# Attention's two stores per sequence, issued by SP among its page requests instead of by GpSimd

## The chip, the cores and the metric

One core of a Trainium2 chip runs the whole program. The metric is the device time of one execution in microseconds. The kernel before took 2566.42 us (median of 3 runs, 2566.22 to 2566.6).

## The reference, cut to what matters

The input x has 64 sequences of 32 tokens and 512 features. Four residual layers follow each other: a linear layer with one of eight weights per sequence, two LoRA layers, and an attention layer. Only the last is touched here. Shortened:

```
q = rope(rmsnorm(x @ Wq.T))        # 32 heads of 128
k = rope(rmsnorm(x @ Wk.T))        # 8 heads
v = x @ Wv.T                       # 8 heads
k_all = concat(k_cache[block_table], k)   # 16 pages of 32 keys + 32 own keys = 544 keys
v_all = concat(v_cache[block_table], v)
probs = softmax(where(valid, q @ k_all.T / sqrt(128), -1e30))
o = probs @ v_all                  # per sequence 128 x (32 heads * 32 tokens)
x = x + o.reshape(64, 32, 4096) @ Wo.T
```

## The kernel before

The attention layer is built by `qkv_attention_and_output` (L1998) from three parts whose programs run one after the other on every engine: `qkv`, `attention` (L1285) and `output_projection` (L1729). Each engine has its own hand-written order of instructions; engines meet only at semaphores.

**Attention.** The sequences s = 0 to 63 are worked off in pairs: `in_pairs` writes the body once for the first pair, once as a loop over pairs 1 to 30, and once for the last pair (i = 31). Each sequence has 8 units, one for each key head; u counts units over all sequences, j within a pair. In a unit TensorE computes the scores of unit u + 2 (`scores`, L1433, six matmuls in three passes of a split fp32), the outputs of unit u - 4 (`outputs`, L1675: eight matmuls with cached values at L1687, two matmul halves with own values at L1690), and the transposes of the probabilities of unit u (`transpose`, L1658). In every fourth unit, the transposes are followed by one of `p_own` (L1670), which first waits for the masked scores of unit u + 2 on VectorE; in every eighth also by the sums' transpose (L1672), so that L1672 marks the end of a sequence's 8 units. VectorE gathers (L1592), masks and takes the maximum (L1403), splits keys and queries into high and low parts (L1378), copies the own probabilities (`copy_own`, L1600), inverts the sums (`invert`, L1607) and copies four heads of outputs out of PSUM (`copy_o`, L1615, which counts `o_ready`, two per sequence). The second of a sequence's two copies is in unit 5 of the next sequence. ScalarE has the exponentials (L1383), the high parts (L1372) and the copies of the transposes (L1558).

**Who asks for what.** SP runs `sync` (L1458): for each sequence 16 requests for key pages of 128 KB (L1350), in four pieces of four pages, each piece once `lo_done` tells that the same buffer's piece of two sequences before has been split. Pieces are split in units 7 (of the sequence before), 0, 2, 3 and 4, so the last piece is asked for after unit 4 and the next sequence's first after unit 7. GpSimd runs `gpsimd` (L1475): for each sequence the queries (L1479, 512 KB), the own keys (L1485), the own values (four requests, L1497, after `pv_done` of unit 3), the value pages as four indirect DMAs of 512 KB each (L1503), and then `store(s - 1)` (L1507): wait for `o_ready`, store the outputs of the sequence before (L1509, 512 KB, 128 rows of 4 KB), wait for `inv_ready`, store its reciprocal sums (L1512, 4 KB).

**Output projection.** Its SP program (L1771) follows attention's on SP. It first waits until four sequences of each parity are stored and until `lo_done` is 6 * 63 (L1790), which is in unit 4 of sequence 61, and then asks for the reciprocal sums of the first tile (`load_inv(0, 0)`, L1778, broadcast to 128 partitions, 1 MB) and for the weights of heads 0 to 3 (`load_w`, L1785, 256 KB each); at `lo_done` 6 * 64, unit 4 of sequence 62, for the first half tile of outputs (`load_o(0, 0)`, L1773, 1 MB) and the weights of heads 4 to 9. The work on these is put into attention's last pair on ScalarE and VectorE by unit number (`HI_AT_STEP`, `LO_AT_STEP`, L1720): weight 0 gets its high part (L1859) on ScalarE at step 6 after that unit's copy of transposes, and its low part (L1863) on VectorE at step 7; the first half tile is scaled at steps 9 to 12 (L1880), split at 10 to 15, and weights 4 to 7 follow at 14 and 15. Step 6 of the last pair is unit 6 of sequence 62. In program order the low part of weight 0 on VectorE stands ahead of `copy_own`, `invert`, `gather` and `mask_and_max` of step 8. The remaining weights wait for `w_split`, eight heads behind.

Of the kernel before, what the change touches and what calls it, by code (L numbers as in the profile page):

```python
# [33 lines left out]
DH, HQ, HK = 128, 32, 8  # L34
# [31 lines left out]


Programs = namedtuple("Programs", "sync gpsimd scalar vector tensor")
Ahead = namedtuple("Ahead", "sync scalar vector tensor")
Kept = namedtuple("Kept", "xt_hi xt_lo w_stage w_loaded after w_hi w_lo w_hi_done w_split")  # L70
Done = namedtuple("Done", "lo_done s_done masked gathered t_done pv_done")
Both = namedtuple("Both", "ident ident_ready step x_stored ps_s ps_pt ps_o ps_y ps_t mm_done normed_ready rotated_ready out_ready stored v_stored")
# [1212 lines left out]
def attention(nc, m, place, both, pool_sems, done, out_ahead, k_pages, v_pages, table, lens, key_at, q_t, k_own, v_own, o_t, inv_t):  # L1285
# [163 lines left out]
    def tensor_ahead(pe, j):  # L1449
# [3 lines left out]
        if j == STEPS:  # L1453

            pe.wait_ge(both.normed_ready, ALL_STEPS - 2)
            scores(pe, 0, 1, 1)

    def sync(sp):  # L1458
        def load_k(s, p):

            for c in PIECE_TURN:
                if c in CACHED:
                    if later(s, 2):
                        sp.wait_ge(lo_done, PIECES * (s - 2) + PIECE_TURN[c])
                    load_pages(sp, s, p, c)

        def pair(i, last):

            if not last:
                for p in range(2):  # L1470
                    load_k(2 * i + 2 + p, p)

        in_pairs(sp, NSEQ // 2, pair)

    def gpsimd(pool):  # L1475
        def load_q(s, p):
            if later(s, 2):
                pool.wait_ge(lo_done, PIECES * (s - 2) + PIECE_TURN[PIECE_Q])
            pool.dma_start(q_raw[p][:, :], q_t[bass.ds(s, 1)].rearrange("s d g x -> s d (g x)"))\  # L1479
                .then_inc(k_loaded[p][PIECE_Q], 16)  # L1480

        def load_own_k(s, p):
            if later(s, 2):
                pool.wait_ge(lo_done, PIECES * (s - 2) + PIECE_TURN[PIECE_OWN])
            pool.dma_start(k_raw[p][:, NPP, :], k_own[bass.ds(s, 1)]).then_inc(k_loaded[p][PIECE_OWN], 16)  # L1485

        def load_own_v(s, p):

            if later(s, 2):
                pool.wait_ge(pv_done, HK * (s - 1))  # L1490
            rows = v_own[bass.ds(s * SEQ, SEQ), :].rearrange("k (g u d) -> k g u d", g=HK // OG, u=OG)
            for u in range(OG):
                if u == 1:
                    pool.tensor_copy(rows_now[:, p, :], row_sb[:, bass.ds(s * (NPP // PPP), NPP // PPP)])\
                        .then_inc(rows_copied, 1)
                    pool.wait_ge(rows_copied, s + 1)
                pool.dma_start(vo_sb[p][u * SEQ:(u + 1) * SEQ, :, u, :], rows[:, :, u, :])\  # L1497
                    .then_inc(own_v_loaded[p], 16)

        def load_v(s, p):  # L1500

            for c in range(NPP // PPP):
                pool.indirect_dma_start(  # L1503
                    v_sb[p][:, c, :], None, v_pages.rearrange("n k x -> (n k) x"),
                    bass.IndirectOffsetOnAxis(ap=rows_now[:, p, c:c + 1], axis=0)).then_inc(v_loaded[p], 16)

        def store(s, p):  # L1507
            pool.wait_ge(o_ready, (HK // OG) * (s + 1))
            pool.dma_start(o_t[bass.ds(s, 1)], o_sb[:, p, :, :].rearrange("p h q -> p (h q)"))\  # L1509
                .then_inc(o_stored[p], 16)  # L1510
            pool.wait_ge(inv_ready, s + 1)
            pool.dma_start(inv_t[bass.ds(s, 1)].rearrange("s (h q) -> (s h) q", h=HK), inv_sb[:, p, :])\  # L1512
                .then_inc(inv_stored[p], 16)

        for p in range(2):
            pool.wait_ge(both.stored[p], 16 * (STEPS // 2) * (NB - 2))
        load_q(0, 0)
        pool.wait_ge(both.stored[0], 16 * ((STEPS // 2) * (NB - 2) + NT // 2 + 1))
        pool.wait_ge(rows_ready, PPP + 2)
        load_own_k(0, 0)  # L1520
        for p in range(2):
            pool.wait_ge(both.v_stored[p], 16 * STEPS // 2)
        pool.wait_ge(both.mm_done, ALL_STEPS)
        pool.memset(mask[:, :, NKEY:NALL], 0.0).then_inc(zeroed, 1)
        load_q(1, 1)
        load_own_k(1, 1)
        pool.memset(vo_sb[0][:, :, :, :], 0.0).then_inc(zeroed, 1)
        pool.wait_ge(zeroed, 2)
        load_own_v(0, 0)
        load_v(0, 0)  # L1530
        for p in range(2):
            pool.wait_ge(both.stored[p], 16 * ALL_STEPS // 2)
        pool.memset(vo_sb[1][:, :, :, :], 0.0).then_inc(zeroed, 1)
        pool.wait_ge(zeroed, 3)

        def pair(i, last):


            for p in range(2):
                s = 2 * i + p  # L1540
                if not last:
                    load_q(s + 2, p)
                    load_own_k(s + 2, p)
                if not (last and p):
                    load_own_v(s + 1, 1 - p)
                    load_v(s + 1, 1 - p)
                if later(s, 1):
                    store(s - 1, 1 - p)

        in_pairs(pool, NSEQ // 2, pair)  # L1550
        store(NSEQ - 1, 1)

    def scalar(act):
        def copy_pt(u, j):
# [102 lines left out]
    def tensor(pe):  # L1657
# [37 lines left out]
        def pair(i, last):  # L1695
# [9 lines left out]
            if last:  # L1705
# [2 lines left out]

        in_pairs(pe, NSEQ // 2, pair)

    return Ahead(sync_ahead, scalar_ahead, vector_ahead, tensor_ahead), Programs(sync, gpsimd, scalar, vector, tensor)

# [7 lines left out]
LO_AT_STEP = {7: ["w0"], 8: ["w1"], 9: ["scale0"], 10: ["scale1"], 11: ["scale2"], 12: ["scale3"], 13: ["o0"], 14: ["o1", "o2"],  # L1722
              15: ["o3", "w2", "w3"], 16: ["w4", "w5", "w6", "w7"]}
HEADS_AHEAD = 8
HALF_1_AT, HALF_1_HI_AT, HALF_1_LO_AT = 9, 11, 14
TILE_1_AT, TILE_1_INV_AT, TILE_1_SCALE_AT, TILE_1_SPLIT_AT = 13, 19, 23, 28


def output_projection(nc, m, base, both, pool_sems, done, x_in, o_t, inv_t, w, x_out):  # L1729
# [38 lines left out]

        return SPT * (n + 1) if isinstance(n, int) and n < 2 else n + 1 + FIRST_TILE_PARTS - 2

    def sync(sp):  # L1771
        def load_o(t, half):
            sp.dma_start(o_sb[half][:, :, :, :].rearrange("p s h q -> p s (h q)"),  # L1773
                         o_t[bass.ds(t * SPT, SPT), :, half * HH * SEQ:(half + 1) * HH * SEQ]
                         .rearrange("s d n -> d s n")).then_inc(o_loaded[half], 16)

        def load_inv(t, half):
            sp.dma_start(inv_sb[:, :, :],  # L1778
                         inv_t[bass.ds(t * SPT, SPT), half * HH * SEQ:(half + 1) * HH * SEQ]
                         .unsqueeze(0).to_broadcast([P, SPT, HH * SEQ])).then_inc(inv_loaded, 16)  # L1780

        def load_w(h):
            if h >= len(stage):
                sp.wait_ge(w_split, h - len(stage) + 1)
            sp.dma_start(stage[h % len(stage)][:, :], w[h // WG][:, h % WG, :]).then_inc(w_loaded[h % len(stage)], 16)  # L1785

        for p in range(2):
            sp.wait_ge(inv_stored[p], 16 * 4)
            sp.wait_ge(o_stored[p], 16 * 4)
        sp.wait_ge(done.lo_done, PIECES * (NSEQ - 1))  # L1790
        load_inv(0, 0)
        for h in range(WG):
            load_w(h)
        sp.wait_ge(done.lo_done, PIECES * NSEQ)
        load_o(0, 0)
        sp.wait_ge(done.s_done, HK * (NSEQ - 1))
        for h in range(WG, HEADS_AHEAD + 2):
            load_w(h)
        sp.wait_ge(scaled, count(0))
        load_inv(0, 1)  # L1800
        sp.wait_ge(done.s_done, HK * NSEQ)
        load_o(0, 1)
        for h in range(HEADS_AHEAD + 2, HQ):
            load_w(h)
            if h == TILE_1_AT:
                sp.wait_ge(split_done, count(0))
                load_o(1, 0)
            if h == TILE_1_INV_AT:
                sp.wait_ge(scaled, count(1))
                load_inv(1, 0)  # L1810
        sp.wait_ge(w_split, HQ)
        sp.dma_start(x_sb[:, :], x_in[0:P, :]).then_inc(x_loaded, 16)
        for p in range(2):
            sp.wait_ge(inv_stored[p], 16 * NSEQ // 2)
            sp.wait_ge(o_stored[p], 16 * NSEQ // 2)

        def pair(i, last):
            for p in range(2):
                t = 2 * i + p
                if not (last and p):  # L1820
                    for half in range(2):
                        if half or later(t, 1):
                            sp.wait_ge(split_done, count(2 * t + half))
                            load_o(t + 1, half)
                            sp.wait_ge(scaled, count(2 * t + half + 1))
                            load_inv(t + 1, half)
                sp.wait_ge(y_ready, t + 1)
                sp.dma_start(x_out[bass.ds(t * P, P), :], y_sb[:, :]).then_inc(y_stored, 16)
                if not (last and p):
                    sp.dma_start(x_sb[:, :], x_in[bass.ds((t + 1) * P, P), :]).then_inc(x_loaded, 16)  # L1830

        in_pairs(sp, NT // 2, pair)
        sp.wait_ge(y_stored, 16 * NT)
# [164 lines left out]
def qkv_attention_and_output(nc, pool_sems, base, shared, both, kept, w_all, lens_tok, inv_freq, step_pos, norm_w, k_pages, v_pages, table, lens, key_at,  # L1998
# [3 lines left out]
    with ExitStack() as ctx:  # L2002
# [17 lines left out]
        with nc.Block(no_gpsimd_drain=True) as block:  # L2020
            @block.sync
            def _(sp):
                proj.sync(sp)
                att.sync(sp)
                out.sync(sp)

            @block.gpsimd
            def _(pool):
# [117 lines left out]
```

## Time and profile before

| | |
|---|---|
| median of 3 runs | 2566.42 us |
| profiled execution | 2564.78 us, span of the core 2563.2 us |
| mean granted TensorE clock | 0.989 |
| TensorE matmul busy | 2422.7 us, 95% |
| VectorE, ScalarE, GpSimd busy | 1777.9, 1606.1, 600.5 us |
| DMA moved | 536.84 MB, mean 209 GB/s |

The profile is one execution. A share of busy time says how full an engine is, not whether it sets the end; for that one reads the chain of waits and the waits by engine. A row of the timeline gives the start, the length, the engine, the line, what is written from what, and in brackets how long the engine was idle before it and what is named as the releaser. "PEld" is TensorE's weight load; "SPq" and "POOLq" are instructions of the queue or sequencer.

### The profile page before, as it was taken

What the parts mean: (1) busy time and instruction counts of PE and PEld (TensorE: products, weight loads), DVE (VectorE), ACT (ScalarE), POOL (GpSimd) and SP (SyncE); (2) the same over time, 40 slices, a digit from 0 to 9 for tenths busy, and PEclk for the clock granted to TensorE, in tenths of its full rate; (3) what the DMA queues carried; (4) which work ended last, traced back from release to release, by engine and by line L of the source; (5) the groups of instructions that cost most, each with busy time, mean ns of one, the idle gap of its engine ahead of it and who ended that gap; (6) DMA issues with size and microseconds to landing.
All of it is one profiled execution on the core that took longest, in us unless ns stands there. A gap on an engine that the chain in (4) does not pass through costs nothing.

```text
span 2563.2 us, 54764 instructions
## 1 busy us (share of the span) xinstructions
PE 2422.7 (95%) x16070; PEld 2185.1 (85%) x16071; DVE 1777.9 (69%) x3668; ACT 1606.1 (63%) x3341; POOL 600.5 (23%) x896
## 2 busy tenths in 40 slices
PE   6899999999999899999999999999999999899999
PEld 4688788888888689999999999999999989788887
DVE  5454439989998777777777777777777777744443
ACT  3233348778777777777777777777777777511111
POOL 1200040000000143444443444443444443000000
PEclk9899999999999899999999999999999999999999
DMA  6622323333334598888788778888887887766564
GB/s 222 177 85 57 128 107 103 99 100 115 99 98 132 159 302 267 267 264 273 270 280 274 267 264 267 278 271 276 274 267 262 273 271 255 278 218 211 209 210 148
DMA packets 377209, 536.84 MB, mean 209 GB/s; under 512 B 49698, under 2 KB 263394, under 8 KB 374306
## 3 DMA queue, kind: packets, MB, share of 16 engines
q1 hardware_dynamic: 304994, 311.62, 38.5%
q0 software_dynamic: 70016, 221.30, 24.8%
q10 hardware_dynamic: 2112, 2.89, 0.4%
q8 instruction: 38, 0.62, 0.1%
q14 instruction: 49, 0.40, 0.0%
HBM read 437.35 MB, written 98.30 MB: 209 GB/s over the span
## 4 chain that ended last, share of the span: by engine, by line
PE 51%; another core or an unknown queue 4%; issue 4%; DVE 4%; ACT 1%; DMA 1%; DVEq 0%; SPq 0%; ACTq 0%
PE both_ps_o L1687 13%; PE both_ps_s L105 9%; PE both_ps_s L103 9%; PE both_ps_s L104 8%; PE both_ps_pt L1664 6%; PE both_ps_o L1690 3%; DVE att_prob L1403 2%; PE both_ps_s L1670 1%; ACT att_prob L1383 1%; DVE att_p_own L1592 0%; DMA out_w_stage<-in_wo 0%; DVE out_w_lo L1863 0%; DMA out_inv<-inv_t 0%; DVE att_shift L1403 0%
## 5 line engine op out<-in xcount | busy, mean ns | idle before, releaser
L1687 PE MATMUL both_ps_o<-att_pt,att_v 128*128 128x128 f32 x4096 | 539.2, 274 | 0.0
L1383 ACT ACTIVATE att_prob<-att_prob,att_shift 128x544 f32<-128x544 f32 x512 | 384.2, 750 | 238.1 <-DVE att_shift L1403 218.1
L1687 PEld LDWEIGHTS both_ps_o<-att_pt,att_v 128*128 128x128 f32 x4096 | 504.0, 191 | 0.0
L1403 DVE CUSTOM_DVE_ANT_0 att_prob<-both_ps_s,att_mask 128x544 f32<-128x544 f32 x512 | 364.1, 711 | 0.3 <-issue 0.2
L103 PE MATMUL both_ps_s<-att_k_hi,att_q_hi 128*128 128x272 f32 x1024 | 339.9, 332 | 6.0 <-DVE att_k_lo L1378 5.0
L1378 DVE TENSOR_TENSOR att_k_lo<-att_k_raw,att_k_hi 128x1024 fp32r<-128x1024 f32 (+1 forms) x320 | 338.0, 1056 | 2.0 <-ACT att_k_hi L1372 1.9
L1558 ACT ACTIVATE att_pt<-both_ps_pt 128x512 f32<-128x512 f32 x512 | 296.8, 580 | 60.7 <-remote 60.1
L1664 PE MATMUL both_ps_pt<-both_ident,att_prob 128*128 128x128 f32 x2048 | 309.2, 274 | 6.2 <-ACT att_prob L1383 4.6
L1592 DVE TENSOR_REDUCE att_p_own<-att_prob 128x32 f32<-128x32 f32 x512 | 89.7, 175 | 324.5 <-remote 159.7
L105 PE MATMUL both_ps_s<-att_k_hi,att_q_lo 128*128 128x272 f32 x1024 | 297.4, 290 | 0.0
L104 PE MATMUL both_ps_s<-att_k_lo,att_q_hi 128*128 128x272 f32 x1024 | 295.3, 288 | 0.0
L1372 ACT ACTIVATE att_k_hi<-att_k_raw 128x1024 fp32r<-128x1024 f32 (+1 forms) x320 | 293.2, 917 | 0.0
L1497 POOL DMA_DIRECT2D att_vo<-v_own x256 | 140.1, 547 | 649.8 <-PE both_ps_o L1690 587.2
L1503 POOL DMA_INDIRECT att_v<-in_v_pages,att_rows_now x256 | 251.9, 984 | 85.9 <-issue 85.9
L1664 PEld LDWEIGHTS both_ps_pt<-both_ident,att_prob 128*128 128x128 f32 x2048 | 242.5, 142 | 6.8 <-ACT att_prob L1383 4.8
L1912 ACT ACTIVATE out_o_hi<-out_o 128x2048 fp32r<-128x2048 f32 x30 | 57.6, 1920 | 265.8 <-DVE out_o L1934 265.8
L103 PE MATMUL both_ps_s<-out_w_hi,out_o_hi 128*128 128x512 f32 x512 | 202.4, 395 | 8.3 <-DVE out_w_lo L1863 4.6
L103 PEld LDWEIGHTS both_ps_s<-att_k_hi,att_q_hi 128*128 128x128 f32 x1024 | 194.8, 190 | 16.3 <-issue 8.8
L105 PE MATMUL both_ps_s<-out_w_hi,out_o_lo 128*128 128x512 f32 x512 | 201.6, 394 | 0.0
L104 PE MATMUL both_ps_s<-out_w_lo,out_o_hi 128*128 128x512 f32 x512 | 201.0, 393 | 0.0
L1690 PE MATMUL both_ps_o<-att_pto,att_vo 128*128 128x128 f32 x1024 | 198.5, 276 | 1.8 <-DVE att_pto L1600 1.8
L104 PEld LDWEIGHTS both_ps_s<-att_k_lo,att_q_hi 128*128 128x128 f32 x1024 | 195.9, 191 | 0.0
(214 smaller groups left out, 5035.5 us busy)
## 6 DMA issues: line engine op xcount, KB each, us to landing
att_k_raw<-in_k_pages SPq DMA_DIRECT2D x1024, 128.0 KB, 4.0
q_t<-qkv_out_t SPq DMA_DIRECT2D x128, 256.0 KB
att_q_raw<-q_t POOLq DMA_DIRECT2D x64, 512.0 KB, 7.2
o_t<-att_o POOLq DMA_DIRECT2D x64, 512.0 KB, 6.9
out_inv<-inv_t SPq DMA_DIRECT2D x32, 1024.0 KB
out_o<-o_t SPq DMA_DIRECT2D x32, 1024.0 KB, 6.6
both_w_stage<-in_w_qkv SPq DMA_DIRECT2D x12, 1024.0 KB, 5.3
l_w_stage<-in_w SPq DMA_DIRECT2D x8, 1024.0 KB, 7.6
```

What stands on the lines that cost most here:

```text
L103: pe.matmul(out, xh, wh, start=start, stop=False)
L104: pe.matmul(out, xh, wl, start=False, stop=False)
L105: return pe.matmul(out, xl, wh, start=False, stop=stop)
L1372: act.activation(hi, raw, ACT.Copy).then_inc(hi_done, 1)
L1378: dve.tensor_tensor(lo, raw, f32(hi), ALU.subtract).then_inc(lo_done, 1)
L1383: act.activation(prob[:, b, :], prob[:, b, :], ACT.Exp, bias=shift[:, b:b + 1], scale=-1.0, accum_out=total[:, j // HK, j % HK:j % HK + 1] ...
L1403: dve.tensor_tensor_reduce(out=prob[:, b, :].rearrange("p (a n) -> p a n", a=2), in0=ps_s[:, j % 2, :, 0:HALF], in1=mask[:, j // HK, :].re ...
L1503: pool.indirect_dma_start(v_sb[p][:, c, :], None, v_pages.rearrange("n k x -> (n k) x"), bass.IndirectOffsetOnAxis(ap=rows_now[:, p, c:c + ...
L1558: act.activation(pt_sb[:, j % OG, :, :], ps_pt[:, j % 2, :, :], ACT.Copy).then_inc(pt_ready, 1)
L1664: mm = pe.transpose(ps_pt[:, j % 2, c, :], prob[:, j % NB_P, c * P:(c + 1) * P], ident[:, :])
L1687: pe.matmul(out, v_sb[p][:, c, h * DH:(h + 1) * DH], pt_sb[:, j % OG, c, :], start=(c == 0), stop=False)
L1690: pe.matmul(out, vo_sb[p][:, g % 2, j % OG, :], pto_sb[:, g % 2, :], start=False, stop=True).then_inc(pv_done, 1)
```

## The change

`store` moves out of `gpsimd` and is written for any engine. SP calls it in attention's pair body: after the page requests for sequence 2i + 2 + p it stores sequence 2i - 2 + p, also in the last pair, where there are no page requests. GpSimd's calls go. The stores of the last two sequences go into SP's program of the output projection: that of sequence 62 after `load_o(0, 1)`, that of sequence 63 after the weight of head 15.

```
+    def store(eng, s, p):
+
+        eng.wait_ge(o_ready, (HK // OG) * (s + 1))
+        eng.dma_start(o_t[bass.ds(s, 1)], o_sb[:, p, :, :].rearrange("p h q -> p (h q)")).then_inc(o_stored[p], 16)
+        eng.wait_ge(inv_ready, s + 1)
+        eng.dma_start(inv_t[bass.ds(s, 1)].rearrange("s (h q) -> (s h) q", h=HK), inv_sb[:, p, :]).then_inc(inv_stored[p], 16)
+
     def sync(sp):
...
         def pair(i, last):
 
-            if not last:
-                for p in range(2):
+            for p in range(2):
+                if not last:
                     load_k(2 * i + 2 + p, p)
+                if later(i, 1):
+                    store(sp, 2 * i - 2 + p, p)
...
                 if not (last and p):
                     load_own_v(s + 1, 1 - p)
                     load_v(s + 1, 1 - p)
-                if later(s, 1):
-                    store(s - 1, 1 - p)
-
         in_pairs(pool, NSEQ // 2, pair)
-        store(NSEQ - 1, 1)
...
+LAST_STORE_AT = 15
...
-    def sync(sp):
+    def sync(sp, store):
...
         sp.wait_ge(done.s_done, HK * NSEQ)
         load_o(0, 1)
+        store(sp, NSEQ - 2, 0)
         for h in range(HEADS_AHEAD + 2, HQ):
             load_w(h)
+            if h == LAST_STORE_AT:
+                store(sp, NSEQ - 1, 1)
```

## Rows read from the trace of the kernel before

**Rows 1.** The page, busy us, share of the span, instructions.
```profile
PE 2422.7 (95%) x16070; PEld 2185.1 (85%) x16071; DVE 1777.9 (69%) x3668; ACT 1606.1 (63%) x3341; POOL 600.5 (23%) x896
```

**Rows 2.** Waits between 930 and 2150 us: us in total, times, longest.
```profile
POOL att_vo L1497 <- PE both_ps_o L1690: 564.7, 59, 10.7
DVE att_p_own L1592 <- remote: 156.8, 54, 3.5
PE both_ps_s L1670 <- DVE att_shift L1403: 69.4, 55, 1.4
```

**Rows 3.** Timeline of GpSimd in one sequence: fourth indirect DMA, stores, queries.
```profile
1521.21 0.94 POOL L1503 DMA_INDIRECT att_v<-in_v_pages,att_rows_now  x1 [0.30 <-issue]
1522.15 0.60 POOL L1509 DMA_DIRECT2D o_t<-att_o  x1
1522.74 0.56 POOL L1512 DMA_DIRECT2D inv_t<-att_inv  x1
1523.30 0.56 POOL L1479 DMA_DIRECT2D att_q_raw<-q_t  x1
```

**Rows 4.** Timeline of TensorE and VectorE, the same sequence and the marks of the one before.
```profile
1503.76 0.27 PE L1672 MATMUL both_ps_s<-both_ident,att_total 128*8 128x128 f32 x1
...
1521.05 0.29 PE L105 MATMUL both_ps_s<-att_k_hi,att_q_lo 128*128 128x272 f32 x1
...
1523.32 0.19 DVE L1592 TENSOR_REDUCE att_p_own<-att_prob 128x32 f32<-128x32 f32 x1 [2.33 <-remote]
...
1524.20 0.33 PE L1670 MATMUL both_ps_s<-both_ident,att_p_own 128*128 128x128 f32 x1 [1.31 <-DVE att_shift L1403]
1524.36 0.27 PE L1672 MATMUL both_ps_s<-both_ident,att_total 128*8 128x128 f32 x1
```

**Rows 5.** The chain of waits, start us and us, one sequence before.
```profile
1500.63 2.06 another core or an unknown queue
```

**Rows 6.** Timeline of TensorE: the marks of the last two sequences.
```profile
2173.83 0.27 PE L1672 MATMUL both_ps_s<-both_ident,att_total 128*8 128x128 f32 x1
...
2191.10 0.27 PE L1672 MATMUL both_ps_s<-both_ident,att_total 128*8 128x128 f32 x1
```

**Rows 7.** Line 989 between 500 and 870 us: SP's stores of queries in the projection.
```profile
L989 SPq DMA_DIRECT2D q_t<-qkv_out_t x90: 372/372/376, 500.6 to 784.4; - x90
```

**Rows 8.** Timeline of SP and VectorE around SP's last page requests of a sequence.
```profile
1516.99 2.38 SPq L1350 DMA_DIRECT2D att_k_raw<-in_k_pages  x4
1517.50 0.69 DVE L1615 COPY att_o<-both_ps_o 128x512 f32<-128x512 f32 x1
1526.17 1.37 SPq L1350 DMA_DIRECT2D att_k_raw<-in_k_pages  x3
```

**Rows 9.** Timeline of SP in the last pair.
```profile
2146.83 0.39 SPq L1778 DMA_DIRECT2D out_inv<-inv_t  x1
2147.28 2.32 SPq L1785 DMA_DIRECT2D out_w_stage<-in_wo  x4
2166.95 0.38 SPq L1773 DMA_DIRECT2D out_o<-o_t  x1
```

**Rows 10.** Timeline of VectorE, ScalarE and TensorE in the last pair.
```profile
2168.01 0.69 DVE L1615 COPY att_o<-both_ps_o 128x512 f32<-128x512 f32 x1
2173.21 0.62 ACT L1859 ACTIVATE out_w_hi<-out_w_stage 128x512 fp32r<-128x512 f32 x1
2174.47 0.28 DVE L1600 COPY att_pto<-both_ps_s 128x128 f32<-128x128 f32 x1
2175.59 0.39 PE L1690 MATMUL both_ps_o<-att_pto,att_vo 128*128 128x128 f32 x2
2178.99 0.69 DVE L1880 TENSOR_TENSOR out_o<-out_o,out_inv 128x512 f32<-128x512 f32 x1
```

**Rows 11.** Window 2173 to 2181 us: length, busy by engine, clock, DMA share, GB/s.
```profile
2173.00:2181.00 8.00, 7.73 (x68) 7.47 (x67) 6.99 (x18) 6.80 (x15) 0.00 (x0) 1.00 1.03 393
```

**Rows 12.** Line 1785 between 2167.3 and 2169.2 us: heads 4 to 7, issue to landing.
```profile
DMA to landing us min/median/max: 6.4/8.5/10.8
```

More of the change, by code:

```diff
@@ L68 @@
 Programs = namedtuple("Programs", "sync gpsimd scalar vector tensor")
-Ahead = namedtuple("Ahead", "sync scalar vector tensor")
+Ahead = namedtuple("Ahead", "sync scalar vector tensor store", defaults=[None])
 Kept = namedtuple("Kept", "xt_hi xt_lo w_stage w_loaded after w_hi w_lo w_hi_done w_split")
@@ L1505, in load_v @@
                     bass.IndirectOffsetOnAxis(ap=rows_now[:, p, c:c + 1], axis=0)).then_inc(v_loaded[p], 16)
[L1507 to L1513, printed above, removed]
         for p in range(2):
@@ L1709, in tensor @@
         in_pairs(pe, NSEQ // 2, pair)
-    return Ahead(sync_ahead, scalar_ahead, vector_ahead, tensor_ahead), Programs(sync, gpsimd, scalar, vector, tensor)
+    return Ahead(sync_ahead, scalar_ahead, vector_ahead, tensor_ahead, store), Programs(sync, gpsimd, scalar, vector, tensor)
 HH = HQ // 2
@@ L2024, in _ @@
                 att.sync(sp)
-                out.sync(sp)
+                out.sync(sp, ahead.store)
             @block.gpsimd
```

## The prediction

> **What bounds the kernel now.** I read the busy shares first: TensorE is busy 2422.7 us, 95% of the span, GpSimd 600.5 us, 23% [rows 1]. The reader should see that GpSimd's share alone promises nothing: work taken from an engine with three quarters of its time free only helps if something waits for that work.
>
> Second, the waits inside attention, 930 to 2150 us [rows 2]. GpSimd waits 564.7 us for TensorE at its own-value requests, about 9.6 us in each of 59 sequences, so it is not behind. TensorE waits 69.4 us in 55 places, always the same: once per sequence, at L1670. VectorE waits 156.8 us in 54 places for a releaser that the profile can't name.
>
> Third, the timeline of one such place [rows 4]. The last score matmul of the unit is at 1521.05 and should be done by 1521.34, but VectorE, which waits for exactly that, starts at 1523.32, 2.0 us later; TensorE then waits 1.31 us for VectorE's mask. The chain of waits puts 2.06 us of the same kind on the path one sequence earlier [rows 5]. So TensorE's completions reach the others late, once per sequence, and the sequence takes 1524.36 - 1503.76 = 20.60 us from mark to mark [rows 4]. The last sequence, in which no value pages are asked for, takes 2191.10 - 2173.83 = 17.27 us [rows 6]; it lacks two units' scores, some 0.75 us each by the spacing of the six matmuls, so 18.8 us is what a sequence takes without the stall. The stall is worth 20.6 - 18.8 = 1.8 us, in 60 sequences about 108 us: the largest thing this change could touch.
>
> Whose stall is it? The late completions arrive in the last stretch of GpSimd's four indirect DMAs and shortly after: the fourth is at 1521.21 to 1522.15, then come the two stores, and VectorE is released at 1523.32, as the queries' request starts at 1523.30 [rows 3, 4]. In the last sequence GpSimd still issues its stores, without indirect DMAs, and there is no stall [rows 6]. I take the indirect DMAs as the cause and the store as a bystander.
>
> **The change part by part.**
>
> *GpSimd loses two requests per sequence,* 0.60 + 0.56 = 1.16 us [rows 3], 64 times, 74 us in all. All lie in front of a 9.6 us wait [rows 2], so on the path they are worth 0. What follows them, the queries and own keys, is asked for 1.16 us earlier; these buffers are used two sequences later, nobody waits. If the cover were gone, it would be 1.16 us a sequence. The value pages are asked for at the same instant as before, since they hang on `pv_done`, so the stall stays where it is. Bounds of what the absence of the stores does to the stall: from 0 to the 1.16 us for which they lie in it. I take 0, by the last sequence, where stores alone stall nothing.
>
> *SP gains the two requests per sequence.* The nearest row is SP's store of 256 KB in the projection, 0.37 us, 90 times alike [rows 7]; twice that is 0.75 us of SP per sequence. SP's fourth piece is asked for from 1516.99 to 1519.37; the second output copy ends at 1518.19, so the wait for `o_ready` is already over when SP gets there, and its next page request that I can see waits for unit 7, about 1525 to 1526 [rows 8]. The store at 1519.4 to 1520.2 therefore lies in 5 us of idle SP: 0 on the path. Queued behind it are the next key pages, which are used more than a sequence later. Had the order been store first, the pages would wait for unit 5. In the projection TensorE's completions are not late beside 90 such stores, so I price SP's stores in the middle of the indirect DMAs at 0 too; no row shows this overlap, so the bounds are from -0.2 us (fewer requests for GpSimd's queue) to +0.3 us a sequence (the stall is pushed out by part of SP's 0.37 us), that is -12 to +18 us over 60.
>
> *Data.* The 512 KB of outputs go out on SP's queue during the values' transfer in place of behind it, so the values land some 1.3 us later (0.52 MB at 393 GB/s, rows 11). They are needed only in unit 4 of the next sequence, well over 5 us after. 0.
>
> *The last pair is where the order costs.* SP now has `store(60)` and `store(61)` ahead of all its output projection work. `store(61)` waits for the second output copy of sequence 61, 2168.01 + 0.69 = 2168.70 [rows 10]. Behind this wait stand the first reciprocal sums and the weights of heads 0 to 3, which before were asked for at 2146.83 to 2149.60 [rows 9]: 22 us later than before. They are wanted soon: ScalarE takes weight 0 at 2173.21 [rows 10]. New times on SP: outputs store at 2168.8, sums at 2169.3, `load_inv` at about 2170.1, weight 0 at 2170.6. Ahead of and with weight 0 on that queue are 0.52 + 1.05 + 0.26 = 1.83 MB, and GpSimd's last value pages, 2.1 MB, start at the same time. Together 3.93 MB at 393 GB/s [rows 11] are 10.0 us, from about 2168.6: 2178.6, plus some 0.3 us to the landing. The rows of before give the same another way: heads 4 to 7 stood behind a 1 MB load on this queue with the same values beside it and took 6.4 to 10.8 us [rows 12]; with 0.52 MB more ahead and a start 1.9 us later than 2166.95, weight 0 corresponds to head 6, at about 2179. I take 2179.1.
>
> What waits for it: ScalarE's high part of weight 0; then on VectorE its low part, and behind that in program order `copy_own`. From the start of the high part to the end of `copy_own` is 2174.75 - 2173.21 = 1.54 us, and TensorE wants that copy at 2175.59 [rows 10], so there is 0.8 us of slack. The delay of TensorE is 2179.1 + 1.54 - 2175.59 = 5.0 us. All engines shift behind it. The next need, scaling the first half tile, was at 2178.99 [rows 10] and goes to 2184; `load_o(0, 0)` needs 0.79 + 1.05 = 1.84 MB after weight 0, 4.7 us, 2183.8: just in time. Bounds: if SP's queue got all the DMA bandwidth, weight 0 would land at 2175.4 (1.83 MB at 393 GB/s after 2170.6) and cost 1.4 us; if it waits like head 7, 10.8 us after 2170.6, 7.4 us.
>
> *The last two stores* join SP's queue between loads that already keep the DMA engines full, with the same bytes as before; SP waits for neither copy by more than 1 us. 0, at most +1.
>
> **Sum.** 0 + 0 + 0 + 5.0 + 0 = +5.0 us on the profiled execution: 2564.78 to 2569.8, its span 2563.2 to 2568.2. The median of the runs lies 1.6 us above that execution, so 2566.42 + 5.0 = 2571.4.
>
> **What the Trainium skill says against it.** "Trainium Kernel Development and Optimization", Key Constraints: requests from SP, ScalarE and GpSimd run on the same 16 DMA engines, and the choice of issuer only saves the issuing sequencer's time. By that rule alone, 1.16 us saved on an idle GpSimd, the sum would be 0 and not +5; it leaves out the place in SP's order. "SBUF — State Buffer", "SBUF: two separate sides", warns of the opposite: descriptors that GpSimd writes starve while VectorE holds the shared port, and SP's requests are free of that, which speaks for a gain; here GpSimd's two requests take 0.60 and 0.56 us with VectorE busy beside them, and nothing waits for them.
>
> **The rivals.**
> A, forecast: the stall unchanged, weight 0 late. +5, by itself +1.4 to +7.4. 60%.
> B, faster: the store is part of the stall. For it: VectorE is released 0.02 us after the sums' store ends [rows 3, 4]. If the completions come through 0.6 us earlier, 60 x 0.6 = -36, with +5 at the end -31: 2535. Against it: the last sequence. It decides from 0.17 us a sequence on (60 x 0.17 = 10). 13%.
> C, slower by more: SP's requests among the indirect DMAs push the stall out. +0.3 us a sequence, +18 with +5: 2589. Against it: the 90 stores of the projection. 12%.
> D, nothing: weight 0 lands by 2174.0, because SP's transfers are served first or the order in the last pair matters less than I read; 2566.4. For it: at the full 393 GB/s it misses that by only 1.4 us. 15%. (This is where the first page's rule ends too.)
>
> **Numbers.** What a measurement of this kernel tells from no change is 0.2%, 5.1 us. A lies across that line, half on each side: 30 same, 30 slower. D is same, B faster, C slower. Allowing for a little of B in small sizes: faster 0.14, same 0.44, slower 0.42. The range leaves out most of B and the upper part of C: 2562 to 2583.
>
> **What would show it.** Marks of L1672 still about 20.5 us apart and TensorE's wait at L1670 still near 70 us: the middle is right. At the end: SP's L1778 and first L1785 after 2168.7 in place of 2146.8, ScalarE's L1859 waiting some 6 us on a DMA of weights, TensorE idle near 5 us at L1690 in the first unit of sequence 63, and no other new wait. The prediction is wrong if the marks move by more than 0.1 us a sequence, or if L1859 does not wait.

## The result, and the profile after

The kernel after takes 2581.59 us (median of 4 runs, 2580.36 to 2582.91), before 2566.32 us beside it: a recorded ratio of 1.0056, 95% interval 1.0044 to 1.0069 (the two medians alone give 1.0060). It is slower by 15.3 us, where 5.0 were forecast. The profiled execution took 2580.36 us, its span is 2578.8 us at a mean clock of 0.987; before's span is 2563.2 us. The difference of the spans, 15.6 us, falls into four stretches, by the marks of the sequences (L1669 after is L1672 before):

| stretch | before | after | difference |
|---|---|---|---|
| up to the first mark of attention | 913.9 | 916.1 | +2.2 |
| marks 1 to 63 (62 sequences) | 1259.9 | 1262.5 | +2.6 |
| last mark to mark (sequence 62 to 63) | 17.27 | 26.85 | +9.6 |
| from the last mark to the end | 372.1 | 373.4 | +1.3 |

The first stretch is no effect of the change: nothing in it is changed, and traces of one kernel differ there by as much (before once more: 916.7, after once more: 914.0).

A mark is the sums' transpose on TensorE, one per sequence; a gather, below, is one of GpSimd's four indirect DMAs of value pages. First the page's line of busy times of after (us, share of the span, instructions), to set beside [rows 1]:

```profile
PE 2424.0 (94%) x16070; PEld 2186.6 (85%) x16071; DVE 1777.1 (69%) x3668; ACT 1604.9 (62%) x3341; POOL 529.3 (21%) x768
```

128 instructions and 71 us are gone from GpSimd. The waits of after between 930 and 2150 us (us in total, times, longest), for [rows 2]:

```profile
POOL att_vo L1506 <- PE both_ps_o L1687: 637.0, 59, 12.5
DVE att_p_own L1589 <- remote: 168.2, 56, 3.4
PE both_ps_s L1667 <- DVE att_shift L1403: 73.5, 58, 2.0
```

GpSimd's 71 us have become 72 us more of its own wait (564.7 before). The wait that the profile can't name is nearly as long as before for each time: 168.2/56 = 3.00 us, before 156.8/54 = 2.90. The timeline of one sequence after, GpSimd, then SP, then TensorE:

```profile
1523.44 0.93 POOL L1512 DMA_INDIRECT att_v<-in_v_pages,att_rows_now  x1 [0.30 <-issue]
1524.37 0.60 POOL L1488 DMA_DIRECT2D att_q_raw<-q_t  x1
...
1522.40 0.70 SPq L1461 DMA_DIRECT2D o_t<-att_o  x1
1523.15 0.71 SPq L1463 DMA_DIRECT2D inv_t<-att_inv  x1
1528.29 1.93 SPq L1350 DMA_DIRECT2D att_k_raw<-in_k_pages  x4
...
1505.97 0.27 PE L1669 MATMUL both_ps_s<-both_ident,att_total 128*8 128x128 f32 x1
1526.43 0.33 PE L1667 MATMUL both_ps_s<-both_ident,att_p_own 128*128 128x128 f32 x1 [1.30 <-DVE att_shift L1403]
1526.60 0.27 PE L1669 MATMUL both_ps_s<-both_ident,att_total 128*8 128x128 f32 x1
```

The reader should see three things. From mark to mark it is 20.63 us (20.60 before). The queries are asked for as soon as the fourth gather is out, and yet TensorE's wait ends at the same distance from that gather's start: 1526.43 - 1523.44 = 2.99 us, before 1524.20 - 1521.21 = 2.99 [rows 3, 4]. And SP's two stores, 0.70 and 0.71 us here where 0.37 was assumed, end at 1523.86, 4.4 us ahead of its next page request.

The last pair is where most of the time went. SP, ScalarE, VectorE and TensorE of after, for [rows 6, 9, 10]:

```profile
2173.43 0.33 SPq L1461 DMA_DIRECT2D o_t<-att_o  x1
2173.81 0.34 SPq L1463 DMA_DIRECT2D inv_t<-att_inv  x1
2174.37 0.36 SPq L1776 DMA_DIRECT2D out_inv<-inv_t  x1
2174.78 3.63 SPq L1783 DMA_DIRECT2D out_w_stage<-in_wo  x4
2178.93 3.61 SPq L1783 DMA_DIRECT2D out_w_stage<-in_wo  x2
...
2186.69 0.63 ACT L1860 ACTIVATE out_w_hi<-out_w_stage 128x512 fp32r<-128x512 f32 x1 [8.63 <-DMA out_w_stage<-in_wo]
...
2187.96 0.28 DVE L1597 COPY att_pto<-both_ps_s 128x128 f32<-128x128 f32 x1
...
2178.58 0.27 PE L1669 MATMUL both_ps_s<-both_ident,att_total 128*8 128x128 f32 x1
2188.30 0.80 PE L1687 MATMUL both_ps_o<-att_pto,att_vo 128*128 128x128 f32 x2 [7.80 <-DVE att_pto L1597]
2205.43 0.27 PE L1669 MATMUL both_ps_s<-both_ident,att_total 128*8 128x128 f32 x1
```

SP asks for weight 0 at 2174.78. After's clock times run 4.75 us later than before's here (2178.58 to 2173.83), so this is 2170.0 in before's time, where 2170.6 was predicted and 2147.28 was before. It lands 11.8 us after its request, at 2186.6; ScalarE waits 8.63 us for it, and TensorE 7.80 us for `copy_own` behind it. TensorE's own matmuls come 2188.30 - 2178.58 = 9.72 us after the mark; before it was 2175.59 - 2173.83 = 1.76. That is 8.0 of the 9.6 us. The windows of after over the idle and what follows it (length; busy of PE, PEld, DVE, ACT, POOL; granted clock; DMA share; GB/s) show the rest:

```profile
2173.40:2186.60 13.20, 6.79 (x57) 6.34 (x56) 1.65 (x7) 2.31 (x6) 2.40 (x3) 0.93 0.98 335
...
2184.00:2186.00 2.00, 0.00 (x0) 0.00 (x0) 0.00 (x0) 0.00 (x0) 0.00 (x0) 0.69 0.95 314
2188.00:2190.00 2.00, 1.70 (x8) 1.71 (x9) 2.00 (x7) 1.24 (x4) 0.00 (x0) 0.50 1.05 395
2190.00:2192.00 2.00, 2.00 (x12) 2.00 (x12) 1.03 (x3) 1.65 (x4) 0.00 (x0) 0.60 1.05 386
2192.00:2194.00 2.00, 2.00 (x20) 2.00 (x19) 1.53 (x6) 1.75 (x4) 0.00 (x0) 1.00 0.94 342
```

TensorE has nothing to do from 2180.5 on. Its granted clock is 0.69 on average from 2184 to 2186 and 0.50 (1.2 GHz) where it resumes at 2188.3; from 2192 on it is 1.00 (2.4 GHz) again. Some 3 us of its work run at half speed, which is the remaining 1.6 us.

### The profile page after: what moved, and what is told of

It reads as the page before. It is cut to its first block, busy times and chain, and to the rows that moved or that the text cites. A ratio compares the mean times of both kernels' runs of the same rounds, so it can differ in the third digit from the quotient of the medians.

```text
span 2578.8 us, 54764 instructions
## 1 busy us (share of the span) xinstructions
PE 2424.0 (94%) x16070; PEld 2186.6 (85%) x16071; DVE 1777.1 (69%) x3668; ACT 1604.9 (62%) x3341; POOL 529.3 (21%) x768
## 3 DMA queue, kind: packets, MB, share of 16 engines
q0 software_dynamic: 58752, 187.48, 21.2%
## 4 chain that ended last, share of the span: by engine, by line
PE 50%; another core or an unknown queue 5%; issue 4%; DVE 4%; DMA 2%; ACT 1%; DVEq 0%; SPq 0%; ACTq 0%
PE both_ps_o L1684 13%; PE both_ps_s L105 9%; PE both_ps_s L103 9%; PE both_ps_s L104 8%; PE both_ps_pt L1661 6%; PE both_ps_o L1687 3%; DVE att_prob L1403 2%; DMA out_w_stage<-in_wo 1%; PE both_ps_s L1667 1%; ACT att_prob L1383 1%; DVE out_w_lo L1864 0%; DVE att_p_own L1589 0%; DMA out_inv<-inv_t 0%; DVE att_shift L1403 0%
## 5 line engine op out<-in xcount | busy, mean ns | idle before, releaser
L1687 PE MATMUL both_ps_o<-att_pto,att_vo 128*128 128x128 f32 x1024 | 198.6, 276 | 8.4 <-DVE att_pto L1597 8.4
```

What stands on the lines that cost most here:

```text
L1687: pe.matmul(out, vo_sb[p][:, g % 2, j % OG, :], pto_sb[:, g % 2, :], start=False, stop=True).then_inc(pv_done, 1)
```

## The experiments

The experiments fell on four chips. On two of them (chips 1 and 2 below) the kernel before takes 2567 to 2568 us, on the other two (3 and 4) 2471 us. The first two profiles are from the first kind. So each kernel is compared with the kernel before on its own chip, and a theory about the 20.5 us sequences can only be tried on the first kind. The expectations of the three runs on chip 3 were written for the first kind; only the difference from before can be set beside them.

**Order of the last pair mended (chip 3).** The store of sequence 60 goes behind `load_inv(0, 0)` and the weights 0 to 3, that of sequence 61 behind `load_o(0, 0)` and the weights 4 to 7; in the middle SP stores as in the kernel after. Nothing of this is on GpSimd.

```diff
@@ attention, sync, pair
-                if later(i, 1):
+                if later(i, 1) and not last:
                     store(sp, 2 * i - 2 + p, p)
@@ output_projection, sync
+        store(sp, NSEQ - 4, 0)
...
-        for h in range(WG, HEADS_AHEAD + 2):
+        for h in range(WG, HEADS_AHEAD):
+            load_w(h)
+        store(sp, NSEQ - 3, 1)
+        for h in range(HEADS_AHEAD, HEADS_AHEAD + 2):
             load_w(h)
```

> The changed kernel with SP's order in the last pair mended: the first reciprocal sums and weights 0 to 3 are asked for before store(60), the first half tile and weights 4 to 7 before store(61). All stores stay on SP. Theory (order): the 7.8 us wait of TensorE at L1687 in the changed kernel and the low clock after it go, some 9.4 us, and ScalarE's wait of 8.6 us for weight 0 is gone: 2581.6 - 9.4 = 2572 us. Rival (the stores' traffic on SP's queue delays the weights wherever they stand): the wait stays at 4 us or more, 2577 to 2582 us.

Measured: 2474.49 us (10 runs) beside 2471.11, ratio 1.001 (1.000 to 1.002). The last sequence is 17.27 us again, and ScalarE has no wait for weight 0. Nearly all other marks are 18.8 us apart on this chip, and so they are in the next run, which in its middle is the kernel before: from mark 1 to mark 63 the two take 1164.7 and 1164.4 us, so SP's stores cost at most 0.3 us there.

**The wait alone (chip 3).** The kernel before, and in SP's program one wait ahead of the output projection's first request. No store moves.

```diff
@@ output_projection, sync
+        sp.wait_ge(o_ready, (HK // OG) * (NSEQ - 2))
```

> The kernel before, stores on GpSimd, with one wait added on SP ahead of the output projection's requests: o_ready of sequence 61. It delays weight 0 as the change does, but moves no store. Theory (order alone suffices): TensorE waits for copy_own in the first unit of sequence 63 for 5 to 7 us, 2566.3 + 6 to 9 = 2572 to 2576 us. Rival (it is the store's data and request time on SP): weight 0 is late by under 2 us, 2566 to 2568 us.

Measured: 2485.02 us (4 runs) beside 2471.11, ratio 1.0049 (1.0032 to 1.0066), +13.9 us, more than the 6 to 9 expected. The last sequence is 29.0 us, 11.8 more than 17.27. SP and TensorE of this run, then two of its windows (columns as above):

```profile
2080.34 2.12 SPq L1786 DMA_DIRECT2D out_w_stage<-in_wo  x4
2082.51 1.25 SPq L1774 DMA_DIRECT2D out_o<-o_t  x1
...
2084.51 0.27 PE L1673 MATMUL both_ps_s<-both_ident,att_total 128*8 128x128 f32 x1
2095.78 0.80 PE L1691 MATMUL both_ps_o<-att_pto,att_vo 128*128 128x128 f32 x2 [9.35 <-DVE att_pto L1601]
2113.53 0.27 PE L1673 MATMUL both_ps_s<-both_ident,att_total 128*8 128x128 f32 x1
...
2097.00:2099.00 2.00, 2.00 (x11) 2.00 (x10) 1.03 (x5) 1.71 (x4) 0.00 (x0) 0.50 1.05 386
2099.00:2101.00 2.00, 2.00 (x15) 2.00 (x14) 1.86 (x5) 0.98 (x3) 0.00 (x0) 0.66 0.85 308
```

The wait is enough to cause the whole loss of the end, with the stores on GpSimd: it is the place in SP's order, not who stores. TensorE idles 9.35 us here, 1.6 more than in the kernel after: weight 0 lands 13.8 us after its request, in after 11.8. The granted clock stays at 0.50 until past 2099, so some 4.6 us of TensorE's work run at half speed, which costs another 2.3: with the idle 11.7 of the 11.8. Why weight 0 lands that much later was not tried.

**Before and after once more, and the weights first (chip 1).** Three runs on one chip of the first kind. The third is the kernel after with one line moved:

```diff
@@ output_projection, sync
-        load_inv(0, 0)
         for h in range(WG):
             load_w(h)
+        load_inv(0, 0)
```

> The kernel before, unchanged, for its trace. If the chip is the one of the first profiles: marks of the sequences 20.3 to 20.6 us apart, 59 idle waits of GpSimd for att_vo of some 9.6 us, about 2566 us. If the chip is the one of the runs e1, e2 and e4: marks 18.8 us apart, no waits of VectorE put down to 'remote' once per sequence, last sequence 17.3 us, about 2471 us.

> The changed kernel, unchanged. Theory T (only the end of attention counts: the last SP requests behind the two stores): attention's middle equal to before's within 3 us, the last sequence +9 to +10 us, output stage +1, so before +10 to +12 us on either chip (2482 beside 2471, or 2578 beside 2566). Rival M (the middle pays too: SP's two more requests per sequence cost up to 0.05 us each sequence, or some 2.6 us in all by the traces compared): +13 to +16 us. If the late completions are what made the middle longer, a chip without them shows the smaller sum.

> The changed kernel with the first four heads' weights of the output stage asked for ahead of the reciprocal-sum load, in the same place of SP's order. Theory T (what TensorE waits for at the end is weight 0, asked for late): the load of 1.05 MB that stood ahead of it takes 2.7 us at 390 GB/s, so TensorE's idle wait of 7.8 us ahead of the output stage goes to about 5 us, and with less time at the low clock behind it the kernel is 3 to 4 us faster than the change (2578 beside 2581.6, or before +8 where before is 2471). Rival R (the wait is for the reciprocal sums or the first attention outputs, which now come after the weights): no gain, 0 to 3 us slower than the change.

Measured: before 2567.03 in this run, 2568.47 over 7; after 2580.76 (4 runs), ratio 1.0045 (1.0028 to 1.0061); weights first 2580.41 (4 runs), ratio 1.0047 (1.0030 to 1.0065). The last sequence takes 17.27, 27.70 and 24.75 us. In the last kernel TensorE idles 1.92 us at L1687:

```profile
2175.65 2.80 SPq L1783 DMA_DIRECT2D out_w_stage<-in_wo  x4
...
2182.10 0.63 ACT L1860 ACTIVATE out_w_hi<-out_w_stage 128x512 fp32r<-128x512 f32 x1 [2.75 <-DMA out_w_stage<-in_wo]
...
2183.71 0.49 PE L1687 MATMUL both_ps_o<-att_pto,att_vo 128*128 128x128 f32 x2 [1.92 <-DVE att_pto L1597]
```

In the trace weight 0 is taken 2182.10 - 2175.65 = 6.45 us after its request, in the kernel after 2186.69 - 2174.78 = 11.91 us. The 1 MB ahead of it on the same queue had cost 5.5 us, which is 192 GB/s: half of the 393 at which I had let it pass [rows 11]. Of that gain the last sequence keeps only 2.95 us, since ScalarE and VectorE next wait for later needs (VectorE 5.3 us for the half tile of outputs). In the whole time the runs don't tell it from the kernel after, whose interval is wider than 3 us; the expected gain of 3 to 4 us is thus seen in the trace and not in the times.

**The order mended, on a chip like the first (chip 2), and once more on one of the other kind (chip 4).**

> The changed kernel with the end of attention in the order of before, as in e1, beside a kernel before of 2566 to 2568 us. Theory T (the end is what costs): last sequence back from 27.7 to 17.3 us; what is left is the middle, where the pairs that were 0.8 us shorter every nine sequences are gone (+4 us in the traces so far), so 2568 to 2573 us, ratio 1.000 to 1.002. Rival M (SP's two more requests cost time in the middle or in the output stage by themselves): 2575 us or more. Where the chip is the quick one (before 2471): 2474, as before.

Measured on chip 4: 2472.35 us (11 runs) beside 2470.68, ratio 1.0003 (0.9994 to 1.0012).

> The changed kernel with the end of attention in the order of before, for the third time, since both times so far fell where a kernel before takes 2471 us and TensorE's completions are not held back (there it was +1.7 and +3.4 us). Where a kernel before takes 2567: theory T: last sequence 17.3 us; 2567 to 2573 us, with what the middle costs (the shorter pairs of sequences that are gone, +2.6 and +4.2 us in the two pairs of traces) as what is left. Rival M (SP's requests cost time beyond that): 2575 us or more. Where before takes 2471: 2471 to 2475.

Measured on chip 2: 2571.64 us (11 runs) beside 2567.32 (15 runs), ratio 1.0019 (1.0010 to 1.0029). The last sequence is 17.27 us. Of the change's 15.3 us (first chip; 12.3 on chip 1), the 9.6 to 10.4 us of the last sequence are gone with the order, and 4.3 us are left on this kind of chip; the kernel after itself was not run on chip 2. The marks say where: between marks 23 and 61 the kernels take

| kernel (chip) | marks 23 to 61, us | last sequence, us |
|---|---|---|
| before (first trace; 1) | 772.5; 772.7 | 17.27; 17.27 |
| after (first trace; 1) | 775.9; 776.5 | 26.85; 27.70 |
| weights first (1) | 776.4 | 24.75 |
| order mended (2) | 776.5 | 17.27 |

All four with SP's stores are 3.2 to 4.0 us longer in this stretch. It is no small cost in every sequence: in kernels with and without SP's stores the usual pair of sequences takes 20.3 + 20.6 us, but in the kernel before one pair in each 9 sequences takes 18.8 + 21.2 or 19.1 + 21.0, 0.8 us less. There GpSimd's second gather starts late, without a wait that the profile names (before, one such place; marks, then GpSimd):

```profile
1443.54 0.27 PE L1672 MATMUL both_ps_s<-both_ident,att_total 128*8 128x128 f32 x1
1462.31 0.27 PE L1672 MATMUL both_ps_s<-both_ident,att_total 128*8 128x128 f32 x1
1483.53 0.27 PE L1672 MATMUL both_ps_s<-both_ident,att_total 128*8 128x128 f32 x1
...
1456.84 1.03 POOL L1503 DMA_INDIRECT att_v<-in_v_pages,att_rows_now  x1 [0.30 <-issue]
1459.82 0.97 POOL L1503 DMA_INDIRECT att_v<-in_v_pages,att_rows_now  x1 [1.95 <-issue]
```

Nine sequences are 108 of GpSimd's requests. In the kernels with SP's stores the shorter pairs stop: after has none behind its third, at about 1361 us. The pauses do not simply stop with the stores: in the last experiment below, which has no store on GpSimd either, GpSimd stands idle 2.1 to 2.3 us ahead of one gather in each 11 sequences, which are 110 requests.

That the 3.2 to 4.0 us are the lost short pairs rests on two things: four such pairs lie in the stretch, and 0.8 us each are 3.2; and where no completion is late, on chips 3 and 4, SP's stores leave the middle within 0.4 us of 1164.4. No run moves the pauses alone, and why GpSimd pauses was not tried. A kernel with SP's stores for sequences 0 to 59 alone, which would price the middle by itself, was not measured.

**The four gathers taken apart (chip 3, then chip 1).** The kernel before, its stores on GpSimd; the first two gathers stand between the own-value requests, each of which waits for one more unit, the fourth stands behind the stores.

```diff
@@ attention, gpsimd, load_own_v
+                if u > 1:
+                    load_v(s, p, u - 2)
+                    if later(s, 2):
+                        pool.wait_ge(pv_done, HK * (s - 1) + u - 1)
@@ attention, gpsimd, pair
-                    load_v(s + 1, 1 - p)
+                    load_v(s + 1, 1 - p, 2)
                 if later(s, 1):
                     store(s - 1, 1 - p)
+                if not (last and p):
+                    load_v(s + 1, 1 - p, 3)
```

> The kernel before with the four indirect DMAs of a sequence spread out: one after each of the own-value requests 2, 3 and 4, which wait one unit longer each, and the fourth after the stores, so that about 2.3 us lie between them; the bytes are the same. Theory (four indirect DMAs 1.25 us apart make TensorE's completions late): the late completions go, a sequence takes 18.5 to 19.0 us in place of 20.45, 60 x 1.5 to 1.9 = 90 to 115 us less: 2451 to 2476 us. Rival (each indirect DMA makes its own delay, whatever the distance): the delays move to other units, where TensorE has more slack or less: 2540 to 2590 us.

Measured on chip 3: 2473.81 us beside 2471.11, ratio 1.0005 (0.9996 to 1.0015). There is no late completion there to remove; it says nothing of the question.

> Kernel before with the four gathers of a sequence asked for one by one between the own-value requests, the last of them after the stores. Where the chip holds TensorE's completions back once per sequence: if the row of four gathers does that, the marks go to 18.8 us apart and the time to 2450 to 2476 us; if each gather does it by itself, marks stay at 20.4 and the time at 2566 within 5. Where the chip does not hold them back: 2471 to 2475 beside 2471, which tells nothing of the cause.

Measured on chip 1: 2471.77 us (4 runs) beside 2568.47, ratio 0.9623 (0.9607 to 0.9639), 97 us faster. All marks but the last are 18.8 us apart. Of VectorE's waits at its gather (L1592 before, L1598 here) between 900 and 2100 us the unnamed releaser is gone, and TensorE's own matmul is what is left. The timeline of GpSimd below it has the four gathers (L1507) of one sequence:

```profile
DVE att_p_own L1598 <- PE both_ps_s L105: 218.1, 282, 1.5
```

```profile
1507.51 1.14 POOL L1507 DMA_INDIRECT att_v<-in_v_pages,att_rows_now  x1 [0.30 <-issue]
1508.65 0.57 POOL L1501 DMA_DIRECT2D att_vo<-v_own  x1
1509.54 1.02 POOL L1507 DMA_INDIRECT att_v<-in_v_pages,att_rows_now  x1 [0.31 <-PE both_ps_o L1696]
1510.55 0.56 POOL L1501 DMA_DIRECT2D att_vo<-v_own  x1
1511.42 1.01 POOL L1507 DMA_INDIRECT att_v<-in_v_pages,att_rows_now  x1 [0.30 <-issue]
1512.43 0.59 POOL L1513 DMA_DIRECT2D o_t<-att_o  x1
1513.02 0.55 POOL L1516 DMA_DIRECT2D inv_t<-att_inv  x1
1513.87 1.69 POOL L1507 DMA_INDIRECT att_v<-in_v_pages,att_rows_now  x1 [0.30 <-issue]
```

The same four gathers and the same bytes, each parted from the next by at least one other request, and no completion is late. So it was the four gathers in a row that held them back, on the chips where anything does; on chip 3 the same row, as far behind the mark as in before (13.3, 14.6, 15.9 and 17.1 us), holds nothing back. The parted gathers start 12.1, 14.1, 16.0 and 18.5 us behind the mark. Two things changed with them, the request between two gathers and their distance (1.9 to 2.4 us in place of 1.3), and this run does not tell which of the two it takes.

**Which part of the row (chip 4).** Two variants of the kernel before: three gathers, the stores, the fourth; and two, the stores, two (`load_v(s + 1, 1 - p, 0, n)` ahead of `store`, the rest behind it, n = 3 or 2).

> Kernel before with the fourth gather of a sequence behind the two stores; the first three stay one right behind the other. If the hold ends with the row (it begins at the second gather and ended 1.9 us after the start of the fourth), it ends one gather earlier, some 1.0 to 1.2 us: marks 19.3 to 19.6 us apart, 2500 to 2520 us. If only a row of four holds: 18.8 us, 2471. If the hold goes with the gathers and not with their row: 20.4, 2566.

> Kernel before with two gathers, then the two stores, then the other two gathers. If the hold lasts from the second gather to the end of the row, two rows of two hold for about 1 us each, which the work ahead mostly covers: marks 18.8 to 19.3 us apart, 2471 to 2503 us. If the hold goes with the gathers and not with their row: 20.4, 2566 us.

Measured: 2474.79 and 2473.57 us (one run each) beside 2470.68, marks 18.8 us apart, as all kernels have them on this chip. Inconclusive: whether a row of two or three already holds completions back stays open. The trace of before has a hint for three: in its shorter pairs one of the two sequences has its last three gathers in a row behind the pause, and the pair is still 2.4 us above twice 18.8 (the usual pair 3.3).

**The change with both mended (chip 4).** Order of the last pair as in the first experiment, no store on GpSimd, gathers parted: two between the own-value requests, the third behind them, the fourth at the start of the next sequence.

> The changed kernel with the end of attention in the order of before, and the four gathers of a sequence one by one: two between the own-value requests, one behind them, the fourth at the start of the next sequence; no store on GpSimd. If a row of gathers is what holds TensorE's completions back, all marks are 18.8 us apart and the kernel takes 2468 to 2476 us, like the spaced kernel with its stores on GpSimd (2471.8). If the stores on GpSimd were needed to part the third gather from the fourth, some of the 1.6 us per sequence comes back: 2480 to 2566 us.

Measured: 2470.35 us (11 runs) beside 2470.68, ratio 1.0001 (0.9992 to 1.0010): no difference, on a chip where none was to be had. It was not run on a chip of the first kind; there the spaced kernel with its stores on GpSimd (2471.8 us) is the best version shown.

## Why the prediction was right in its mechanism and short in its size

- **GpSimd loses two requests, worth 0.** Right: 71 us of work became 72 us of wait.
- **SP gains two requests, worth 0 in a sequence (bounds -0.2 to +0.3).** Right for the usual sequence, 20.63 us against 20.60, though a request took 0.70 us and not 0.37. Rival C's push of the stall did not come: from mark 1 to mark 63 the marks moved by 0.04 us a sequence (0.07 on chip 1), inside the 0.1 that the prediction gave itself.
- **The store is a bystander of the stall, the gathers are its cause.** The first half is shown by the trace after (2.99 us from the fourth gather to TensorE's restart with and without the stores), which ends rival B. The second is shown by the spaced kernel, with the limit named there, and 18.8 us a sequence, read off the last one, is what it measured. It gained 97 us, where the prediction had priced the stall at about 108.
- **A term of the sum left out.** The middle is 2.6 us longer in the profiled pair (3.2 to 4.0 us from mark 23 to 61 in all kernels with SP's stores). I had read one usual sequence and taken it for all 60; a list of all marks would have shown the shorter pairs of before, which could be lost. The term was put at nothing, with bounds of -12 to +18 us for another reason.
- **Weight 0 late, +5.0.** The right place, the right order and the request within 0.6 us; the size was too small: +9.6. Rival D is out. Two parts were mis-sized. The first is the landing: 3.93 MB at 393 GB/s made 10.0 us, but the window 2173.4 to 2186.6 ran at 335 GB/s and moved 4.4 MB, so more than the bytes up to weight 0 had passed before it was whole; it took 13.2 us. In before's time weight 0 landed at 2181.8, where 2179.1 was forecast, and TensorE's idle became 7.8 us. The weights-first run prices the 1 MB ahead of weight 0 at 5.5 us. My upper bound of 7.4 us took head 7's 10.8 us from request to landing [rows 12]; weight 0 took 11.8. The second is the clock: after the idle some 3 us of TensorE's work ran at 1.2 GHz, which cost another 1.6 us, a term that I did not have.
- **The last two stores, 0 to +1.** +1.3 in this trace from the last mark to the end, within what the same stretch differs between traces of the kernel before (371.9 and 372.1) and others (372.2 to 374.9): not told apart.
- **The sum.** 9.6 + 2.6 + 1.3 = 13.5 us of the 15.6 in the spans; the other 2.2 (rounded) stand ahead of attention. The time lies in the range, near its upper end, and that is in part luck: the range reached to 2583 for the sake of rival C, which did not come, while the forecast mechanism by itself was bounded at +7.4, 2573.8. By the rule of the Trainium skill, "Trainium Kernel Development and Optimization", Key Constraints, that issuing from several engines only saves sequencer time, it would have been 0; the run with the wait alone shows what the rule leaves out, +13.9 us by the place in one engine's order.

## What to carry to other kernels

When a store moves to another queue, look first at what stands behind it where the loop ends: a wait that is free sixty times can stand ahead of the next stage's first loads once. Price a load behind others by what its own queue gets while other queues move data (here half of the rate), and add the low clock after a long idle of TensorE (here 1.6 us after 7.8, and 2.3 after 9.35). And where an engine's completions come late without a named releaser, try parting the requests that GpSimd issues at that time before moving any one of them; compare only kernels that ran on the same chip.

## What the runs showed of the hardware

- The kernel before takes 2567 to 2568 us on two chips (2566 in the first profiles, whose chip is not on record) and 2471 on two others, at the same mean clock (0.988 for the kernel before on chip 1, 0.988 for the order mended on chip 4). The late completions, once per sequence, are nearly all of it: from mark 1 to mark 63 the kernel before takes 1259.9 us, the wait alone on chip 3 1164.4, which is 95 of some 96 us. With the gathers parted, a chip of the first kind gives 2471.8.
- SP's requests are not of one length. From the start of a sequence's outputs store to the start of its sums' store it is 0.38 to 0.40 us behind the loop, in the last pair and the output projection, 0.54 in the loop on chip 3, and 0.75 in most sequences of the loop in after. The weights' requests of the last pair took 0.91 each (3.63 for four) and once 2.91 us while the values and weights were under way.
- GpSimd pauses 1.7 us more than usual at its second gather each 108 requests, on both kinds of chip (before, and the wait alone), and on the kind with late completions those pairs of sequences were shorter, not longer. With ten requests a sequence it is each 110 (the last experiment).
